# Output projection in the bank of the small products, and the shared network four units behind its batch

## The reference

```python
q, k, v = (split_heads(holo_linear(xn, ...)) for each)      # 16 heads of 16
attn = softmax(einsum('bhqd,bhkd->bhqk', q, k) * 16 ** -0.5)
out = einsum('bhqk,bhkd->bhqd', attn, v)                    # back to 256 columns
attention = holo_linear(out, basis_o, phase_o, amp_o)
# holo_linear(x) = (x @ basis.T) @ (amp * cos(phase)).T, through 32 harmonics
# network: 8 experts of width 352, the best two of each row weighted with 2.5 * share,
#          and for every row the shared network of width 704:
shared = (silu(xn @ sw_gate) * (xn @ sw_up)) @ sw_down
```

## Time and profile before

| what | us |
|---|---|
| median of 3 runs (lowest, highest) | 1097.99 (1097.19, 1098.69) |
| the profiled execution | 1095.13 |
| its span, first to last instruction | 1093.4 |
| PE busy in it | 966.9 (88%) |
| DVE, ACT, POOL busy | 647.7 (59%), 541.8 (50%), 334.2 (31%) |
| mean granted clock of TensorE | 0.916 |

### The profile page before, as it was taken

The page is one execution under the profiler, slowest core; times in us unless marked ns, Lnnn a source line. Parts: engine busy times, 40 slices in busy tenths (PEclk is TensorE's granted clock), DMA queues, the critical chain, the costliest instruction groups (busy, mean ns, idle before and its releaser), DMA issues.

```text
span 1093.4 us, 18008 instructions
## 1 busy us (share of the span) xinstructions
PE 966.9 (88%) x5673; PEld 643.4 (59%) x5674; DVE 647.7 (59%) x1063; ACT 541.8 (50%) x824; POOL 334.2 (31%) x307
## 2 busy tenths in 40 slices
PE   2783669999999995989999999999999999999995
PEld 1681669999999993324455454454454454554554
DVE  6657783433443435656766757757757767667522
ACT  2323224444444443455756646646746647556551
POOL 1000252222222211502522524504605506426252
PEclk9755579999999997568999999999999999999998
DMA  8688262222222224533645655554644734524120
GB/s 250 230 291 241 101 193 74 68 68 74 69 67 77 67 59 119 168 106 99 183 130 145 185 140 138 176 146 127 185 123 146 195 104 144 160 63 111 47 60 19
DMA packets 94798, 140.65 MB, mean 129 GB/s; under 512 B 18568, under 2 KB 51920, under 8 KB 93712
## 3 DMA queue, kind: packets, MB, share of 16 engines
q1 hardware_dynamic: 88208, 122.01, 37.9%
q0 software_dynamic: 6528, 17.83, 5.8%
HBM read 79.96 MB, written 54.85 MB: 123 GB/s over the span
## 4 chain that ended last, share of the span: by engine, by line
PE 50%; issue 18%; POOL 17%; DVE 8%; ACT 3%; DMA 2%; SPq 1%; POOLq 0%; DVEq 0%; ACTq 0%
PE bank L1072 7%; PE st_pair L1054 7%; PE s_pair L1054 6%; PE bank L1229 6%; POOL h_T L698 5%; POOL y_b L709 5%; POOL y_b L715 4%; PE st_pair L1175 4%; PE bank L1187 4%; PE s_pair L1131 3%; DVE top L1528 3%; PE bank L1062 2%; PE bank L965 2%; POOL ao_T L704 2%; PE bank L1164 1%
## 5 line engine op out<-in xcount | busy, mean ns | idle before, releaser
L1528 DVE TENSOR_REDUCE top<-s_pair 128x2 f32<-128x1024 f32 x256 | 313.3, 1224 | 195.4 <-PE s_pair L1131 193.2
L881 ACT ACTIVATE prob<-st_pair 128x1024 f32<-128x1024 f32 x256 | 261.0, 1019 | 192.2 <-PE st_pair L1175 191.3
L698 POOL TENSOR_TENSOR h_T<-h_f,h_T 128x512 fp32r<-128x512 f32 (+1 forms) x48 | 62.1, 1295 | 373.2 <-ACT h_T L863 373.0
L672 POOL DMA_INDIRECT xg<-xn_rows,token_of x72 | 71.8, 998 | 307.2 <-PE bank L1037 182.4
L1175 PEld LDWEIGHTS st_pair<-q_rows,k_rows 50*128 50x128 f32 x512 | 50.0, 191 | 178.3 <-ACT prob L881 130.3
L1175 PE MATMUL st_pair<-q_rows,k_rows 50*128 50x512 f32 x512 | 133.9, 519 | 17.1 <-ACT prob L881 12.4
L1187 PE MATMUL bank<-prob,v_ones 128*32 128x512 f32 x1024 | 144.2, 637 | 0.0
L1164 PE MATMUL bank<-xT_b,w_sh 128*128 128x512 f32 x528 | 143.2, 407 | 0.0
L1131 PE MATMUL s_pair<-k_rows,q_rows 48*128 48x512 f32 x512 | 118.2, 455 | 11.8 <-DVE top L1528 11.5
L1164 PEld LDWEIGHTS bank<-xT_b,w_sh 128*128 128x128 f32 x528 | 93.7, 188 | 31.1 <-issue 12.3
L1072 PE MATMUL bank<-w_exp,c_hT 128*128 (+1 forms) x648 | 94.9, 291 | 1.0 <-ACT c_y L814 1.0
(11 more groups left out here) (204 smaller groups left out, 1195.6 us busy)
## 6 DMA issues: line engine op xcount, KB each, us to landing
qk_rows<-qk_hi SPq DMA_DIRECT2D x56, 256.0 KB
q_rows<-qk_rows SPq DMA_DIRECT2D x64, 192.0 KB
k_rows<-qk_rows SPq DMA_DIRECT2D x56, 192.0 KB
expert_rows<-c_y SPq DMA_DIRECT2D x72, 128.0 KB, 1.7
xn_T_split<-x_T SPq DMA_DIRECT2D x8, 1024.0 KB, 4.6
xT_b<-xn_T_split SPq DMA_DIRECT2D x32, 256.0 KB, 4.9
qk_rows<-qk_lo SPq DMA_DIRECT2D x28, 256.0 KB
x_all<-in_L_attn_x_dram SPq DMA_DIRECT2D x8, 512.0 KB, 6.2
```

What stands on the lines that cost most here:

```text
L672: pool.indirect_dma_start(xg[s % 4][:, :], None, xn_dram, bass.IndirectOffsetOnAxis(token_of[:, s:s + 1], 0)).then_inc(c_x[s % 4], 16)
L698: pool.tensor_tensor(h_T[0:m, LO, f, :], h_f[f % 2][0:m, :], h_T[0:m, HI, f, :].bitcast(F32), ALU.subtract).then_inc(p_h, 1)
L881: act.activation(prob[kt % 2][:, 2 * jp:2 * jp + 2, :].rearrange("p j l -> p (j l)"), st_pair[:, :], ACT.Exp, scale=HD ** -0.5).then_inc(a ...
L1528: dve.tensor_reduce(top[g % 2][:, :, jp, qt], s_pair[:, :].rearrange("p (i k) -> p i k", i=2), AX_X, ALU.max).then_inc(d_max, 1)
```

## The change

FIRST becomes 4. The gates and ups of batch b now begin in slot 1 of b itself, and its downs come in slot 0 of b+1. "out" of batch b-1 stays in step 7 of slot 1. The 64-column part is now made second of the six (ORDER, BOTH), so it stays in step 5 of slot 1. Downs no longer hold the output projection: project_o is two pairs of matmuls into m_bank, in steps 1 and 3 of slot 2, and DVE adds each pair by itself (add_out, 128x512) in steps 2 and 4. turn_max for slot 3, in step 5 of slot 2, waits for the second addition. project_values of the next batch moves from slot 2, step 2 to slot 3, step 3, where it waits for r_lo. The last batch's own way, with four banks, goes. The first down waits for hidden_low part by part. SP stores and loads o_b at other places, and POOL's list is written anew.

```diff
-        FIRST = 12
+        FIRST = 4
+        ORDER = (0, SFT - 1) + tuple(range(1, SFT - 1))
+        BOTH = 1
...
             u = g * 4 + t // 2
             c, i = b if u >= FIRST else b - 1, (u - FIRST) % 16
+            if i == 3:
+                return ("out", c - 1, 0) if there(c - 1) else (None, None, None)
             if not there(c):
                 return None, None, None
-            if i <= 10:
-                return ("gate", "up")[i % 2], c, i // 2
-            return ("out", c, 0) if i == 11 else ("down", c, i - 12)
+            if i < 3:
+                return (("gate", c, 0), ("up", c, 0), ("gate", c, BOTH))[i]
+            return (("gate", "up")[i % 2], c, i // 2) if i < 12 else ("down", c, i - 12)
...
             def store_out(b, h):
-                wait(sp, d_dn, b * TPB + 2 * h + 2)
+                wait(sp, d_po, b * 2 + h + 1)
...
             for b in range(NB):
                 hidden_low(b, 0)
-                ao_low(b, 0)
+                hidden_low(b, 1)
+                if there(b - 1):
+                    ao_low(b - 1, 1)
                 for n in range(4):
                     scale_y(b, n)
-                hidden_low(b, 1)
+                hidden_low(b, 2)
                 for n in range(4, 8):
                     scale_y(b, n)
-                hidden_low(b, 2)
+                hidden_low(b, 3)
+                add_pair(b)
+                hidden_low(b, 4)
                 add_y(b)
-                hidden_low(b, 3)
+                ao_low(b, 0)
                 for n in range(4):
                     if there(b + 1):
                         gather_y(b + 1, n)
-                hidden_low(b, 4)
-                ao_low(b, 1)
+                hidden_low(b, 5)
                 for n in range(4, 8):
                     if there(b + 1):
                         gather_y(b + 1, n)
-                hidden_low(b, 5)
+            ao_low(NB - 1, 1)
...
             def turn_max(b, g):
...
                 if g == 0:
-                    wait(pe, d_r, b + 2) if more else wait(pe, a_mt, (b - 1) * NG + 4)
+                    wait(pe, a_v, b * 2 + 1)
...
                 else:
-                    wait(pe, a_v, (b + 1) * 2 + 1) if more else wait(pe, a_mt, b * NG + 3)
+                    wait(pe, d_po, b * 2) if b else wait(pe, a_mt, b * NG + 3)
...
             def project_values(b, half):
...
                     wait(pe, r_in, b * 96 + 48)
-                    wait(pe, d_qk, b * 4 + 4)
-                    wait(pe, a_mt, (b - 1) * NG + 3)
+                    wait(pe, d_r, b + 2) if there(b + 1) else wait(pe, a_mt, (b - 1) * NG + 4)
...
             def down_shared(b, t):
...
                 if t == 0:
                     wait(pe, d_hf, b * SFT + SFT)
-                    wait(pe, p_h, b * SFT + SFT)
...
+                    if t == 0 and i % 3 == 0:
+                        wait(pe, p_h, b * SFT + q + 1)
...
+            def project_o(b, h):
+
                 wait(pe, d_res, b + 1)
...
+                wait(pe, d_po, b * 2 + h) if h else wait(pe, a_mt, min((b + 1) * NG + 3, NB * NG))
+                for n in range(2):
+                    t = 2 * h + n
+                    ins = pe.matmul(m_bank[:, n * D:(n + 1) * D], ro[:, t * P:(t + 1) * P], w_rows[:, 3, :], start=True, stop=True)
+                ins.then_inc(b_po, 1)
...
             def low_rank_o(b):
                 wait(pe, p_ao, 2 * b + 2)
-                wait(pe, d_hf, b * SFT + SFT - 1)
+                wait(pe, d_hf, (b + 1) * SFT + 1) if there(b + 1) else wait(pe, d_dn, NB * TPB)
...
+            def add_out(b, h):
+                wait(dve, b_po, b * 2 + h + 1)
+                wait(dve, d_dn, (b + 1) * TPB)
+                dve.tensor_tensor(o_b[:, 2 * h:2 * h + 2, :], m_bank[:, :].rearrange("p (t d) -> p t d", t=2), o_b[:, 2 * h:2 * h + 2, :],
+                                  ALU.add).then_inc(d_po, 1)
...
-                    if g == 2 and t == 2 and there(b + 1):
+                    if g == 3 and t == 3 and there(b + 1):
                         project_values(b + 1, 0)
...
+                    if g == 2 and t in (1, 3) and there(b - 1):
+                        project_o(b - 1, t // 2)
```

More of the change, by code:

```diff
@@ L401, in build_program @@
         ht_bank = [bank[6], bank[7]]
-        def down_bank(b, t):
-            return bank[t] if b == LAST else (g_bank, u_bank)[t % 2]
         @block.sync
@@ L524, in load_xT @@
                 wait(sp, b_g, (b - 2) * SFT)
+                wait(sp, b_gu, (b - 2) * (SFT - 1))
                 for k in range(KT):
@@ L608, in slot @@
                     load_xT(b + 2, HI)
-                if g == 3 and there(b - 1):
-                    store_out(b - 1, 1)
+                if g == 3 and there(b):
+                    load_x_b(b)
                 if there(pb) and pg % 2:
@@ L618, in slot @@
                     load_low_rank(b + 2)
+                if g == 2 and there(b - 1):
+                    store_out(b - 1, 0)
                 if there(nb):
@@ L628, in slot @@
                 if g == 2 and there(b - 1):
-                    store_out(b - 1, 0)
-                if g == 3 and there(b):
-                    load_x_b(b)
+                    store_out(b - 1, 1)
             slots(slot)
@@ L690, in _, with hidden_low @@
                 pool.wait_ge(c_st[i], 16 * (NS // 4))
-            def hidden_low(b, f):
-                m = P if f < SFT - 1 else SF_LAST
-                n = b * SFT + f
+            def hidden_low(b, q):
+                m, f = rows_of(q), ORDER[q]
+                n = b * SFT + q
                 wait(pool, a_hh, n + 1)
                 wait(pool, b_dn, b * TPB)
-                pool.tensor_tensor(h_T[0:m, LO, f, :], h_f[f % 2][0:m, :], h_T[0:m, HI, f, :].bitcast(F32),
+                pool.tensor_tensor(h_T[0:m, LO, f, :], h_f[q % 2][0:m, :], h_T[0:m, HI, f, :].bitcast(F32),
                                    ALU.subtract).then_inc(p_h, 1)
@@ L851, in max_rows, with tanh, hidden_high @@
                 act.activation(top_T[g % 2][:, :], m_bank[0:8, :], ACT.Copy).then_inc(a_mt, 1)
-            def tanh(b, f):
-                wait(act, b_g, b * SFT + f + 1)
-                wait(act, p_h, b * SFT + f - 1)
-                m = P if f < SFT - 1 else SF_LAST
-                act.activation(h_f[f % 2][0:m, :], g_bank[0:m, :], ACT.Tanh, scale=0.5).then_inc(a_th, 1)
-            def hidden_high(b, f):
-                wait(act, d_hf, b * SFT + f + 1)
+            def tanh(b, q):
+                wait(act, b_g, b * SFT + q + 1)
+                wait(act, p_h, b * SFT + q - 1)
+                m = rows_of(q)
+                act.activation(h_f[q % 2][0:m, :], g_bank[0:m, :], ACT.Tanh, scale=0.5).then_inc(a_th, 1)
+            def hidden_high(b, q):
+                wait(act, d_hf, b * SFT + q + 1)
                 wait(act, b_dn, b * TPB)
-                m = P if f < SFT - 1 else SF_LAST
-                act.activation(h_T[0:m, HI, f, :], h_f[f % 2][0:m, :], ACT.Copy).then_inc(a_hh, 1)
+                m = rows_of(q)
+                act.activation(h_T[0:m, HI, ORDER[q], :], h_f[q % 2][0:m, :], ACT.Copy).then_inc(a_hh, 1)
             def values_out(b, half):
@@ L896, in low_rank_o_high @@
                 wait(act, b_res, b + 1)
-                wait(act, b_dn, b * TPB)
+                wait(act, b_po, b * 2)
                 act.activation(ro[:, :], u_bank[0:96, :], ACT.Copy).then_inc(a_res, 1)
@@ L919, in slot @@
                     what, c, i = unit_before(b, g, t)
-                    if what == "up" or what == "gate" and i == SFT - 1:
+                    if what == "up" or what == "gate" and i == BOTH:
                         hidden_high(c, i)
@@ L1193, in low_rank @@
                 wait(pe, xT_in, (b + 1) * 64)
-                wait(pe, a_v, (b - 1) * 2 + 1)
                 wait(pe, a_mt, (b - 2) * NG + 4)
@@ L1599, in slot @@
                         low_rank_o_low(c)
+                    if g == 2 and t in (2, 4) and there(b - 1):
+                        add_out(b - 1, t // 2 - 1)
                     if g == 3 and t == 2 and there(b + 2):
```

81 lines of the change are left out of this document (40 added, 41 removed).

## The result

The changed kernel takes 1133.25 us (median of 6 runs, 1131.64 to 1138.98), the kernel before beside it 1096.74 (6 runs). The ratio is 1.0348, 95% interval 1.0312 to 1.0383: 36.5 us slower between the medians, where 33.9 were forecast. The ratios leave out runs that lie over 1.5% above the fastest of the same kernel. The profiled execution took 1138.98, with a span of 1137.0 against 1093.4. Its 43.6 us more are: the first exponential 2.05 later (442.03 against 439.98), the slots with exponentials 668.5 in place of 614.1, 54.4 more, and 26.4 in place of 39.3 behind the last exponential, 12.9 less.

What follows compares the result with a forecast made beforehand. From about 500 us PE's written order was taken as the bound, its waits paid in full. 51.4 us lost less 17.5 gained made 33.9 slower: 1129.0 for the profiled execution, 1131.9 for a median, range 1103 to 1146.

Steps and rivals of the forecast that it cites:

- The likeliest case: The forecast itself: all waits A to E paid, 33.9 us slower, a median of 1131.9 us; given 42%.
- the page's row of the clock: Sign named for the profile after: clock digits under 9 in the loop.
- Wait A: Slot 1, step 7: low_rank_o waits for POOL's second ao_low, now behind a hidden_low; 3.2 us net, seven times, 22.4 lost.
- Wait B: PE's clock falls in the idle of about 4 us before low_rank_o; five of seven fall, 1.6 each, 8.0 us lost.
- Wait C: Slot 2, step 5: turn_max waits for DVE's second addition of the output projection; 1.0 us, seven times, 7.0 lost.
- Wait D: Slot 3, step 3: the moved project_values waits for DVE's r_lo; 0.7 us, six times, 4.2 lost.
- Wait E: The first down's last three matmuls wait for POOL's last hidden_low, behind four gathers; 1.4 us, seven times, 9.8 lost.
- Start: Slots 0.1 and 0.2: the first gate group raises the clock, giving 19.8 and 16.9 us; 2.4 us gained.
- Small gain: The first down's old wait for POOL goes, since a gate stands there now; 2.6 us gained.
- Tail: After the last exponential only down remains: 25.5 us in place of 39.3, less 1.3 for a low clock; 12.5 us gained.
- The rival in which POOL keeps up: POOL's order costs nothing, so A, B and E go, 40.2 us: 1091.7 us, faster than before; 12%.

Runs made afterwards that it cites:

- e2: Changed kernel with 18 matmuls of unread result put on PE ahead of low_rank_o's wait for ao_low; 1128.89 us, ratio 1.021 to 1.031.
- e1: Changed kernel with POOL's ao_low put back ahead of the 64-column hidden_low, nothing else; 1104.18 us, ratio 1.0024.
- e7: Changed kernel with waits A, C and D repaired: ao_low ahead, add_out at its step's head, project_values behind the up; 1095.99 us, ratio 0.990 to 1.000.
- e10: e7 with the last hidden_low ahead of the gathers, four of them moved to the next batch's slot 1 behind ao_low; 1079.71 us, ratio 0.9869.
- e3: Kernel before with one thing changed, POOL's second ao_low put behind the 64-column hidden_low; 1127.87 us, 2.2% slower.
- e4: Changed kernel with ao_low ahead and the last hidden_low ahead of all eight gathers, C and D left; 1146.1 us, one run.
- e11: As e10, but all eight gathers in one train in slot 1 behind the second ao_low; 1080.56 us, ratio 0.983 to 0.994.
- e6: Changed kernel with waits A, C, D and E all repaired, the eight gathers in one train in slot 0; 1143.61 us, ratio 1.030 to 1.041.
- e13: e6 with each gather from batch 1 on fetching 128 bytes a row in place of 1024; 1140.97 us, one run.

## Why the prediction was right

The likeliest case came, with every wait at its place and released by whom the prediction said. Of its signs one failed: the page's row of the clock has no digit under 9 in the loop. Its sizes per batch, from the slots of the table:

| step | forecast, us | measured, us | from |
|---|---|---|---|
| Wait A | 3.2 x 7 = 22.4 | 3.22 x 7 = 22.5 | e2 less e1, slot 1 |
| Wait B | 5 falls x 1.6 = 8.0 | 7 falls x 2.01 = 14.1 | after less e2, slots 1 and 2 |
| Wait C | 1.0 x 7 = 7.0 | 1.00 x 7 = 7.0 | e1 less e7, slot 2 |
| Wait D | 0.7 x 6 = 4.2 | 0.80 x 6 = 4.8 | e1 less e7, slot 3 |
| Wait E | 1.4 x 7 = 9.8 | 1.25 x 7 = 8.8 | after less e10, slot 0 |
| Start | -2.4 | +1.3 | slots 0.1 and 0.2 |
| Small gain | -2.6 | -4.1 | what is left of 54.4, not measured by itself |
| Tail | -12.5 | -12.9 | 26.4 against 39.3 |

The first exponential, 2.05 us later in the profiled execution, lies ahead of all edits and was no step. For the small gain e10 gives another figure: without waits A to E its four slots sum to 77.29 us, against 77.71 before, 0.42 a batch or 2.9 in seven.

**A.** The working held to a tenth of a microsecond: ACT's high part, two POOL instructions, and PE standing 4.01 us. e3 shows that POOL's order makes it, with nothing else of the change. The rival in which POOL keeps up failed as its counter-argument said: the time was set by when the input came, and a POOL busy for 31% of the span doesn't help.

**B is the term that was mis-sized.** The clock fell in all seven waits, not five, and each fall costs 2.0, not 1.6. The working held an unbroken idle against a stretch of the start that was only sparse, and nothing in its rows said that two of seven would be spared. What I had left out of the price is how long the half rate lasts behind the wait: besides low_rank_o (2.88 against 1.54 us, 1.3) come a pair of scores at 0.80, a pair at 0.63 and eight small products at 1.43, where 0.50, 0.40 and 1.06 stand at full rate, another 0.9. The Trainium skill (TensorE: Matmul & The Clock Gate, section "HAM oscillation — how this bites in real kernels") counts half of the throttled time. Here the throttled stretch from 993.48 to 998.80 is 5.3 us long, and 2.0 of them, about four tenths, are lost, where half would be 2.7. The rule agrees roughly with this trace once the stretch's own length goes in; the page's 1.67 us of throttled time, which gave my 5.8, was that of another kernel.

**C and D** are as worked out from the earlier trace rows. In slot 4.2 of after DVE's order and the late turn_max, and in slot 4.3 the late project_values:

```profile
837.31 0.68 DVE L1568 SCALAR_TENSOR_TENSOR h_f<-h_f,bank 128x512 f32<-128x512 f32 x1
837.91 0.69 DVE L1583 TENSOR_TENSOR o_b<-bank,o_b 128x512 f32<-128x512 f32 x1
...
838.74 0.60 PE L1160 MATMUL bank<-ident_f,top_parts 128*8 128x128 f32 x4 [1.12 <-DVE o_b L1583]
...
853.42 0.68 DVE L1572 TENSOR_TENSOR r_lo<-bank,r_hi 96x512 fp32r<-96x512 f32 x1
...
854.25 0.63 PE L1229 MATMUL bank<-w_rows,r_v 96*128 96x128 f32 x4 [0.79 <-DVE r_lo L1572]
```

The price of add_out, put at 0.7 from hidden_shared, is 0.69. turn_max waits 1.19 us a time (8.3 in 7), my 1.2, and its repair gives back 1.00. The difference is the size of the slack of 0.2 that I took off, though no run tests the slack by itself.

**E** was right in kind: the last hidden_low stands behind add_y, ao_low and four gathers, and the last three matmuls of the first down wait for it. The profile has 0.99 us of wait a time (6.9 in 7), and slot 0 is 1.25 shorter without it. What the sum did not have is that the plain repair makes slot 0 6.5 us longer than the wait had it (30.44 in e4, 23.94 in e1).

**Start** has the wrong sign in the profiled execution, and half of it is chance. Slots 0.1 and 0.2 together take 36.8 to 36.9 us in six of the twelve kernels with this start, against 39.1 before: 2.3 gained, my 2.4. In the other six they take 39.4 to 40.7, after among them. In after the clock rose with the first gate as expected, and fell again in step 7, which has no group in slot 0.1:

```profile
467.41 2.46 PE L1182 MATMUL bank<-xT_b,w_sh 128*128 128x512 f32 x6
469.80 0.50 PE L1193 MATMUL st_pair<-q_rows,k_rows 50*128 50x512 f32 x2
...
483.56 0.79 PE L1193 MATMUL st_pair<-q_rows,k_rows 50*128 50x512 f32 x2 [2.45 <-ACT prob L894]
```

That empty step was not in my working. It costs the quick traces the same (e10 has 2.46 us there and a pair at 0.79 behind it); they differ in that slot 0.1 is at full rate from its beginning (18.55 us, clock 1.00, against 21.24 at 0.82). So the 2.4, where it came, came by another way than mine: slot 0.1 1.2 shorter than my 19.8, slot 0.2 1.4 longer than my 16.9. Even the same code goes both ways: e3 has the start of the kernel before, and takes 15.1 and 15.1 us where that one's profile has 21.05 and 18.06.

**Tail.** low_rank_o was due 17.1 us after the last exponential and came 16.8 after it (1127.40 less 1110.57), at half rate (2.44) as counted. normalise took 0.69 with POOL idle, in place of 2.17 beside POOL. The end came at 26.4 in place of 25.5 plus the 1.3 for the clock.

**The sum.** Losses 57.2 in place of 51.4 (5.8 more, 6.1 of them in B), the start 3.7 worse, the other gains 1.9 better, and 2.05 ahead of everything: 9.7 over the 33.9 for the profiled execution, which is the slowest of the six runs. The medians are 36.5 apart, 2.6 over the forecast. That nearness is partly luck: the profiled execution of after lies 5.7 us over its median and that of before 1.6 under its own, and these 7.3 us cover most of the 9.7. No trace of a median execution says which steps are smaller there.

**What stays open** is what holds up TensorE's signals, and ACT and DVE with them. That POOL's gathers have a part in it is shown by e4 against e7 and by e10 and e11; how they act on TensorE isn't. The long waits come with the train of eight gathers in slot 0 (e4, e6, e13), where SP's transfers of q, k and the sums also run, and don't depend on bytes (e13). In slot 1, step 6 the same train does nothing (e11). Neither slot 0 nor eight gathers is needed for the shorter ones: e3 has waits of 2.2 to 4.2 us behind four gathers in step 1 of slot 1, where before, with the same train, has none. Whether it is SP's transfers that the gathers meet, the matmuls that PE has under way, or something else, was not tried.

## What to carry to other kernels

In an engine's hand-written list, put the instruction that the bound engine waits for ahead of one whose own input comes late: here two swapped instructions on an engine with two thirds of its time free cost 26 us (e3) to 35 us (e1). A wait of 4 us on TensorE, 3.2 of them on the path, cost 2.0 more here, because the clock fell with it, so price the wait and everything behind it at half rate. Repair waits one at a time, and read the timeline after each: four repairs at once gave 1144 us, and the same four with half of the gathers moved to where POOL was idle gave 1080.

## What was not expected of the hardware

- Behind a train of eight gathers on POOL (0.95 us each with 0.30 between) in slot 0, four semaphore updates of TensorE came 3.1 to 5.8 us late and within 0.2 us of each other (e4, e6, e13). ScalarE and VectorE, which wait for them, went on together 1.8 to 3.0 us after the last gather. No instruction of TensorE, ScalarE or VectorE reads what the gathers write. The Trainium skill (SBUF — State Buffer, section "SBUF: two separate sides") says that within the engine side only the port pair shared by VectorE and GpSimd is contended, and that ScalarE never waits on anyone. No run here contradicts it: ScalarE's idle of 5.38 us in e6 was for TensorE's signal, not for a port, and that page doesn't explain why the signal was late.
- With the clock at full speed in the start (granted clock 1.00 in e3, against 0.54 and 0.72 before), slots 0.1 and 0.2 of the old order take 30.2 us in place of 39.1. The start's time is set more by which level the clock has there than by any edit in it.
